# Two steps of each row maximum taken ahead of the attention product, scores taken ahead of maxima, and the sums' product put behind the fold

## The reference

```python
qn = layernorm(x, ln_q_g, ln_q_b)
q = qn @ Wq * scale                       # 16 heads of 64
k, v = jnp.split(media @ Wkv, 2, axis=-1)
sim = jnp.einsum('bhid,bhjd->bhij', q, k)
sim = jnp.where(media_mask[:, None, None, :], sim, neg_inf)
attn = jax.nn.softmax(sim, axis=-1)
out = jnp.einsum('bhij,bhjd->bhid', attn, v)
x = x + jnp.tanh(attn_gate) * (out @ Wo)
h = layernorm(x, ln_ff_g, ln_ff_b)
x = x + jnp.tanh(ff_gate) * (jax.nn.gelu(h @ W1, approximate=False) @ W2)
```

```python
memory_proj = jnp.einsum('bme,de->bmd', memory, W_mem)
attn = softmax(hidden_states @ memory_proj^T / sqrt(D))
gate = sigmoid(concat(hidden_states, attn @ memory_proj) @ W_gate + b_gate)
out = rmsnorm(hidden_states + gate * (attn @ memory_proj), norm_w)
```

## Time and profile before

| | |
|---|---|
| median of 3 runs | 861.2 (860.52 to 861.25) |
| the profiled execution, whole | 861.04 |
| its span, first to last instruction | 859.2 |
| TensorE busy | 822.5 (96%), granted clock 0.998 of full speed |
| TensorE weight loads busy | 695.9 (81%) |
| VectorE busy | 615.8 (72%) |
| ScalarE busy | 465.2 (54%) |
| GpSimd busy | 419.3 (49%) |
| row maxima, line 960 | 256 times, mean 989 ns |
| exponentials, line 675 | 192 times, mean 1026 ns |
| GpSimd additions, line 491 | 128 times, mean 2398 ns |
| chain that ended last | PE 76%, DVE 12%, POOL 5%, ACT 4% |

### The profile page before, as it was taken

One profiled execution on the slowest core, in us unless ns is written; L12 is line 12 of the kernel. 1 busy time (PEld: TensorE's weight loads), 2 busy tenths in 40 slices (PEclk: granted clock), 3 DMA queues, 4 the chain that ended last, 5 costly groups with the idle time before them and its releaser, 6 DMA issues.

```text
span 859.2 us, 18530 instructions
## 1 busy us (share of the span) xinstructions
PE 822.5 (96%) x7905; PEld 695.9 (81%) x7905; DVE 615.8 (72%) x992; ACT 465.2 (54%) x727; POOL 419.3 (49%) x205
## 2 busy tenths in 40 slices
PE   4999999999999999999999999999999999998986
PEld 3787888888888888888888888888888778997775
DVE  6956789867657888677578986775787756445375
ACT  4755665657446656575366665753555552125352
POOL 2445565655625656556256565562588685000001
PEclk9999999999999999999999999999999999999999
DMA  9100001000000010000000000000100500000201
GB/s 280 31 2 2 2 2 39 2 2 2 2 1 2 2 39 2 2 2 2 1 2 2 2 1 2 2 2 1 50 2 2 169 2 1 2 1 1 77 1 49
DMA packets 20560, 16.81 MB, mean 20 GB/s; under 512 B 1008, under 2 KB 19456, under 8 KB 20480
## 3 DMA queue, kind: packets, MB, share of 16 engines
q1 hardware_dynamic: 20192, 15.38, 6.0%
q10 hardware_dynamic: 288, 0.27, 0.1%
HBM read 14.59 MB, written 1.05 MB: 18 GB/s over the span
## 4 chain that ended last, share of the span: by engine, by line
PE 76%; DVE 12%; POOL 5%; ACT 4%; issue 2%; DMA 1%; ACTq 0%; POOLq 0%; DVEq 0%
PE psum L1357 20%; PE psum L375 17%; PE psum L1371 15%; PE psum L1326 6%; PE psum L1282 4%; POOL acc L491 3%; PE psum L1386 3%; PE psum L1147 3%; PE psum L1221 2%; DVE mx L960 2%; DVE ot L990 2%; DVE k_lo L949 1%; PE psum L1377 1%; ACT v L658 1%; PE psum L1212 1%
## 5 line engine op out<-in xcount | busy, mean ns | idle before, releaser
L491 POOL TENSOR_TENSOR acc<-acc,ring 128x1024 f32<-128x1024 f32 x128 | 306.9, 2398 | 18.7 <-POOL acc L486 0.5
L960 DVE TENSOR_REDUCE mx<-psum 128x2 f32<-128x800 f32 (+2 forms) x256 | 245.3, 989 | 83.6 <-PE psum L1326 71.8
L675 ACT ACTIVATE ring<-psum 128x1024 f32<-128x1024 f32 x192 | 196.9, 1026 | 65.7 <-PE psum L1357 59.4
L486 POOL TENSOR_TENSOR acc<-ring 128x1024 f32<-128x1024 f32 x32 | 76.6, 2394 | 255.5 <-ACT ring L675 255.5
L1371 PE MATMUL psum<-ring,v 128*64 128x256 f32 (+1 forms) x1664 | 186.7, 381 | 1.8
L1371 PEld LDWEIGHTS psum<-ring,v 128*64 128x64 f32 (+1 forms) x1664 | 116.6, 137 | 60.8 <-DVE k_lo L949 3.9
L1357 PE MATMUL psum<-nm,maskrow 64*128 64x256 f32 (+1 forms) x832 | 123.9, 294 | 0.6 <-ACT ring L675 0.6
L1357 PE MATMUL psum<-q_hi,k_hi 64*128 64x256 f32 (+1 forms) x832 | 117.2, 278 | 0.0
L1357 PE MATMUL psum<-q_lo,k_hi 64*128 64x256 f32 (+1 forms) x832 | 116.9, 277 | 0.0
L1357 PE MATMUL psum<-q_hi,k_lo 64*128 64x256 f32 (+1 forms) x832 | 116.8, 277 | 0.0
L667 ACT COPY od<-psum 128x512 f32<-128x512 f32 x32 | 18.8, 586 | 158.5 <-PE psum L1377 158.5
(11 more groups left out here) (164 smaller groups left out, 1473.5 us busy)
## 6 DMA issues: line engine op xcount, KB each, us to landing
nat<-in_ctx_dram SPq DMA_DIRECT2D x7, 768.0 KB
w<-in_L_xattn_W_dram SPq DMA_DIRECT2D x2, 1024.0 KB, 6.2
wo<-in_L_xattn_Wo_dram SPq DMA_DIRECT2D x1, 1024.0 KB, 10.3
out_dram<-t_res SPq DMA_DIRECT2D x8, 128.0 KB, 1.7
mask<-in_mask_BxS_bk_dram SPq DMA_DIRECT2D x4, 200.1 KB, 7.2
nat<-in_ctx_dram SPq DMA_DIRECT2D x2, 384.0 KB, 7.2
ring<-in_L_xattn_Wkv_dram SPq DMA_DIRECT2D x2, 384.0 KB, 6.8
wq<-in_L_xattn_Wq_dram SPq DMA_DIRECT2D x1, 768.0 KB, 7.3
```

The costliest lines, as they stand in the source:

```text
L486: nc.gpsimd.tensor_tensor(acc[:, :, :, :], ring[:, 0, :, :, :], ring[:, 1, :, :, :], ALU.add)\
L491: nc.gpsimd.tensor_tensor(acc[:, :, :, :], acc[:, :, :, :], ring[:, g, :, :, :], ALU.add)\
L675: nc.scalar.activation(ring[:, g, :, :, :], score_set[m % 2].rearrange("p (h i q) -> p h i q", h=2, i=2), ACT.Exp).then_inc(S["p_ready"], 1)
L960: nc.vector.tensor_reduce(mx[:, t, :, c], pair[:, :, 0:min(c1, KEYS) - c0], axis=AX.X, op=ALU.max).then_inc(S["m_max"], 1)
```

## The change

Five edits in the written order, and what follows from them in the waits:

1. M steps 0 and 1 of the pair after next are taken out of the row phase and put at the end of the full-array phase, behind R and ahead of the attention product. They no longer use aux banks but the two score sets, each in the set of the score group that comes next there; step 0 waits for all exponentials of the pair before, and score groups 0 and 1 wait for the maxima of these steps.
2. The row phase begins with S groups 0 and 1, then M steps 2 and 3, then S group 2, and so on in turn.
3. F, the sums' product, goes from the end of the full-array phase to directly behind U, the fold.
4. In LAST, `z.0 z.1` hang on N of pair 7 instead of F of pair 5; the other extras keep their places, `d.0 d.1` behind U of pair 6 among them.
5. `side_banks` leaves the moved steps out of its count; in FIRST the steps of pair 9 keep aux banks.

```diff
 def row_phase(j):
-    out = [("M", j + 1, 0), ("S", j, 0), ("M", j + 1, 1)]
-    for g in range(1, KEY_GROUPS):
+    out = [("S", j, 0), ("S", j, 1), ("M", j + 1, 2)]
+    for g in range(2, KEY_GROUPS):
         out += [("M", j + 1, g + 1), ("S", j, g)]
     return out
...
-    return out + [("F", j - 1), ("R", j + 1)]
+    return out + [("R", j + 1)] + [("M", j + 2, step) for step in range(EARLY_STEPS)]
...
 def column_phase(j):
-    return [("U", j)] + items(COLUMN_EXTRAS.get(j, "")) + [("A", j), ("D", j)]
+    return [("U", j), ("F", j - 1)] + items(COLUMN_EXTRAS.get(j, "")) + [("A", j), ("D", j)]
...
-LAST_EXTRAS = {("A", 2): "s.0", ("A", 3): "s.1", ("A", 4): "s.2", ("A", 5): "n.0 n.1 n.2", ("F", 5): "z.0 z.1",
+LAST_EXTRAS = {("A", 2): "s.0", ("A", 3): "s.1", ("A", 4): "s.2", ("A", 5): "n.0 n.1 n.2", ("N", 7): "z.0 z.1",
                ("U", 6): "d.0 d.1", ("R", 7): "w.0", ("S", 7, 6): "h.0.0 h.0.1 g.0.0 g.0.1", ("A", 7): "h.1.0 e.0.0 e.0.1",
...
+    def in_score_sets(order, item):
+        if item[0] != "M" or order is FIRST and item[1] == PAIRS + 1:
+            return False
+        return item[2] < EARLY_STEPS or order is FIRST and item[1] == PAIRS
+
+    def score_set_of(item):
+        return (item[2] if item[1] == PAIRS else (item[1] - 1) * GROUPS + item[2]) % 2
...
                         if in_score_sets(order, item):
-                            if item[2] > 1:
-                                upto(pe, "m_max", b, n * SCORE_STEPS + item[2] - 1)
-                            pair = score_set[item[2] % 2].rearrange("p (h n) -> p h n", h=2)
+                            if order is FIRST and n == PAIRS:
+                                if item[2] > 1:
+                                    upto(pe, "m_max", b, n * SCORE_STEPS + item[2] - 1)
+                            elif item[2] == 0:
+                                upto(pe, "p_ready", b, (n - 1) * GROUPS)
+                            pair = score_set[score_set_of(item)].rearrange("p (h n) -> p h n", h=2)
...
                         upto(pe, "p_ready", b, m - 1)
+                        if g < EARLY_STEPS and in_score_sets(order, ("M", n + 1, g)) and not (order is LAST and n == PAIRS - 1):
+                            upto(pe, "m_max", b, (n + 1) * SCORE_STEPS + g + 1)
```

More of the change, by code:

```diff
@@ L18 @@
 SCORE_STEPS = 8
+EARLY_STEPS = 2
 AHEAD = {"S": PAIRS, "M": PAIRS, "N": PAIRS, "R": PAIRS, "K": PAIRS, "L": PAIRS, "U": PAIRS, "A": PAIRS, "D": PAIRS, "E": PAIRS,
@@ L80, in first_order @@
     behind_scores = items("V.4.4 V.4.5 V.4.6 G.5 Q.5")
-    others = [i for i in ahead if i not in early + behind_scores]
+    scores = items("M.9.0 M.9.1") + [i for g in range(1, KEY_GROUPS) for i in (("M", PAIRS + 1, g + 1), ("S", PAIRS, g))]
+    others = [i for i in ahead if i not in early + scores + behind_scores]
     cut = others.index(("N", PAIRS + 1)) + 1
-    return early + others[:cut] + behind_scores + others[cut:]
+    return early + scores + others[:cut] + behind_scores + others[cut:]
 def cross_attention_kernel(nc, x, media, media_mask, ln_q_g, ln_q_b, Wq, Wkv, Wo, attn_gate,
@@ L123, in side_banks @@
         for item in BODY:
+            if in_score_sets(BODY, item):
+                continue
             if item[0] == "M":
@@ L137, in cross_attention_kernel @@
                            (0, 1, 2, 3, 0, 1, 2, 3, 0, 1, 2, 3, 0, 1, 3, 0, 1, 2, 3, 0, 0, 2, 1, 3)))
+    FIRST_BANKS.update({("M", PAIRS + 1, i): BANK["M", PAIRS + 1, i + EARLY_STEPS] for i in range(EARLY_STEPS)})
     def bank_of(order, item):
-        return FIRST_BANKS.get(item, BANK[item]) if order is FIRST else BANK[item]
+        return FIRST_BANKS[item] if order is FIRST and item in FIRST_BANKS else BANK[item]
     def banks_of(order, item):
@@ L613, in attention @@
                     kind, n = item[0], item[1]
-                    if kind in USES_BANK:
+                    if kind in USES_BANK and not in_score_sets(order, item):
                         bank = aux[bank_of(order, item)]
@@ L956, in attention @@
                         if in_score_sets(order, item):
-                            pair = score_set[item[2] % 2].rearrange("p (h n) -> p h n", h=2)
+                            pair = score_set[score_set_of(item)].rearrange("p (h n) -> p h n", h=2)
                         else:
-                            pair = aux_pair[BANK[item] // 2]
+                            pair = aux_pair[bank_of(order, item) // 2]
                         nc.vector.tensor_reduce(mx[:, t, :, c], pair[:, :, 0:min(c1, KEYS) - c0],
```

6 lines of the change are left out of this document (2 added, 4 removed).

## The result

The changed kernel takes **880.4 us** (879.8 to 882.9, four runs) against 861.2 (860.5 to 861.3, four runs) for the kernel before: ratio 1.0228, 95% interval 1.0216 to 1.0240. It is 2.3% slower; the forecast was 861.6 with a range up to 868.0. The profiled execution took 882.9, the slowest of the four and 2.5 above their median; its span is 881.1, 21.9 more than the 859.2 before. One run of experiment 2, 924.1 at a granted clock of 0.873 where all others of this study have 0.99 or more, is left out of its median.

The account below looks back on a forecast made before the run. TensorE, busy 96% of the span, was taken as the bound, with loads held by VectorE's maxima and key splits. Terms -13.4 - 2.9 - 1.4 + 14.2 + 3.9 = +0.4 us gave 861.6 as a median; range 855.5 to 868.

Parts of the forecast that it names:

- regular phases: 19 row phases of 8.26 to 8.28 us, forecast to shorten to 7.81, a gain of 0.46 each.
- held ones: 3 row phases whose next phase's bank waits for the last maximum; forecast 8.53, gaining 0.45 to 0.56 each, 1.4 together.
- late ones: 7 row phases where VectorE reaches the first maximum late; beyond the regular gain, their excess over 8.27 goes: -2.9 us.
- pair 6's row phase: Last touched row phase, 9.55 us before; its fold, and with it product D, was forecast 1.4 sooner.
- The switch: Two maxima steps between R and A, with tile-shape changes on both sides: 0.57 us each, +14.2 in all after cover.
- the cover: In 15 places where A waits for the key split, the steps hide 0.19 of that hold, costing 0.38 instead of 0.57.
- free switch: Rival on the two steps between R and A: shape change almost free, 0.30 a pair, 853.6 us; chance 0.15.
- 0.69: Rival on the two steps between R and A: they cost 0.69, what the column shape costs, 865.3 us; chance 0.20.
- The trap at the end of the last batch: Moved product behind fold and splits delays ScalarE's copy and pair 7's exponentials by 3.0 to 4.0 us; taken as +3.9.
- Hidden at nothing: Two early VectorE maxima (about 2 us), score groups 0 and 1 waiting for them, and the product behind the fold cost nothing.
- new D wait: GpSimd's sum starts 0.7 us sooner in each phase, so no added wait of D for it was expected.
- D of pair 6: Last touched phase: TensorE waits for GpSimd's sum, which starts sooner, so fold and D come 1.4 us sooner.

Follow-up runs that it names:

- experiment 2: Changed kernel with the last batch's two token splits hung behind the sums' product of pair 5 instead of the fold of pair 6: 876.4 us, ratio 1.0179.
- experiment 1: Changed kernel with the negation of the maxima made by a negated tensor_reduce instead of a product with -1: 862.97 us, ratio 1.0019.
- experiment 3: Changed kernel with the negation as a reduction and the last batch's token splits behind the sums' product of pair 5: 857.44 us, ratio 0.9956.
- experiment 4: Kernel before the change with only the negation made by a reduction: 860.83 us, ratio 0.9997.

## Why the prediction was wrong

**What held.** Bounds and durations of the row phase were right load by load; regular phases 0.48 against 0.46 forecast, held ones 8.50 to 8.52 against 8.53, late ones at 7.79 to 7.81 but for the first with 7.91, pair 6's row phase 1.1 shorter. The switch took 0.56 to 0.57 each, thirty times; with the cover of 2.6 seen in experiments 1 and 3 that is 14.3 (14.2 forecast). The rivals of a free switch and of 0.69 are out. The trap at the end of the last batch was real, and experiment 2 takes it away; that it cost 4.3 against 3.9 is partly luck, since the wait was 3.4, in the forecast's 3.0 to 4.0 but below the 3.9 taken, and the other 1.0 is the half clock behind it, which the forecast did not have. With the negation not held, the kernel measures 862.97, 1.4 above the forecast, most of it in pair 7 (5.0).

**The step that failed** is "Hidden at nothing", together with a zero that was never written down: that full-array phases keep their length. It priced what the moved items do and left every item that had not moved at its old duration. It even had the cause in hand, "it starts 0.7 us sooner in each phase than before, so I see no new D wait", and asked that shift one question only. The other was: which VectorE work beside the additions reads SBUF alone, and where does it start? That is N's negation, 0.23 in the trace of before. The order couldn't show it, since N had not moved against anything on its own engine; the trace of before could: 385.52 for the negation, 385.55 for the addition, a margin of 0.03 us on one side of which it costs 0.23 and on the other over 2. Shown in its place: the negation takes 2.16 in the median, the full-array phases 19.1 more, and with that one instruction in another form both are gone (experiment 1).

**What it cost where.** The negation took 1.8 to 2.0 more in 28 of the 32 pairs, and VectorE's queue is in order, so everything that TensorE needs behind it is late. Phases that transpose the context have least slack (nine transposes: 5.68 to 7.44 in one batch and 8.97 in two, where the clock fell behind a hold of 2.15 on `mt`; four: 6.13 to 7.80 in two of three batches), then those with keys and values alone (5.42 to 6.50), while a phase that opens with queries absorbs most (7.17 to 7.38). Together 19.1, where -2.6 of cover would have stood. The forecast had no term for the clock either; in this trace it falls behind the long holds alone, and in experiments 1 and 3, without those holds, no full-array phase has it.

Here I had weighed a rule half. The Trainium skill, SBUF — State Buffer, "Who interferes with whom" (its "single rule"), was applied to VectorE's product with two SBUF inputs alone. The same section names `tensor_scalar`, with `copy` and `cast`, among the operations that can enter a two-port mode, when their operands allow it, and then contend with GpSimd, whoever issues first holding the other off for a whole instruction, and says that `tensor_reduce` never contends on trn2. This case's trace agrees with both: 2.16 behind an addition and 0.23 ahead of it for the one, 0.285 to 0.290 in every pair for the other (experiments 1, 3 and 4). The other direction hardly shows: GpSimd's addition that starts 0.03 behind the negation took 2.47, and the same one behind the reduction of experiment 4 took 2.41.

**D of pair 6** was said to come 1.4 sooner. In experiment 3 pair 6's row phase is 1.1 shorter and its column phase 0.35 (7.78 to 7.43), the whole -0.4 of that account: 1.5 together. In the changed kernel itself the column phase gives 1.6, but the full-array phase ahead of it grew by 1.7. The 0.9 ahead of the first row phase is not the change's as far as the record shows: in five variants with the same order there it lies between -0.7 (experiment 2) and +0.5 (experiment 1). Why it scatters was not looked into.

## What to carry to other kernels

When a change shifts when GpSimd starts, list every operation on VectorE that reads and writes SBUF alone and can overlap it, moved or not, and read from the trace how far each starts from the nearest GpSimd operation; a margin of hundredths of a microsecond is one that a change can undo, even where it has held in 30 pairs out of 32. A short operation of that kind at the head of an in-order queue is priced at its neighbour's remaining time, and if it has a form that isn't held, take that form first. And move the early work only in the phases whose own account is positive.

## What the runs showed of the hardware that was not expected

- A `tensor_scalar` of 128x128 fp32 from SBUF to SBUF takes 0.227 undisturbed and up to 2.19 when it starts inside a GpSimd addition of 2.39; it then ends about 0.08 after that addition. A negated `tensor_reduce` with the same result takes 0.285 to 0.290 in all pairs, with additions running (experiments 1 and 4).
- A cast of 128x512 from SBUF on VectorE is held in the same way, in the kernel before too: the second one (L780 there, L792 in the changed kernel) starts 0.39 behind a GpSimd subtraction of 1.6 and takes 1.50 to 1.52 in all eleven traces, and it ends 0.28 after that. Two later casts of the same line and shape, with no GpSimd work beside them, take 0.42. No run took GpSimd's operation away from the held one, so this is a comparison of places and not an experiment.
- TensorE's granted clock fell to half, for 3.4, behind holds of 2.15, 2.16 and 3.76, and stayed full behind another of 2.16 at the same place one batch later. Where it fell, a phase with nine transposes took 1.5 more. So a hold of some 2 us can cost more than itself, and not in each execution alike.
